# Output stage of an attention and MXFP4 linear layer: VectorE's order and one maximum moved to GpSimd

## What is computed

```python
x = _layernorm(x + _L0_attn_ref(x, ...), axis=-1)          # 32 heads of 16, causal, RoPE, bias, softmax offset
x = _layernorm(x + _L0_ffn_ref(x, ffn_weight, ffn_bias), axis=-1)

def _quant_dequant_mxfp4(x):                               # on blocks of 32 along the last axis
    amax = jnp.max(jnp.abs(xb), axis=-1, keepdims=True)
    exp = jnp.floor(jnp.log2(jnp.maximum(amax, tiny))) - 2.0
    scale = jnp.where(amax > 0, jnp.exp2(exp), 1.0)
    q = jnp.clip(xb / scale, -6.0, 6.0)
    aq = jnp.abs(q)
    lsb = jnp.where(aq < 2.0, 0.5, jnp.where(aq < 4.0, 1.0, 2.0))
    return jnp.round(q / lsb) * lsb * scale

def _L0_ffn_ref(input, weight, bias):
    return quant_dequant(input) @ quant_dequant(weight).T + bias
```

## Time and profile before

| | us |
|---|---|
| median of 3 runs | 1631.46 |
| lowest and highest of them | 1629.03, 1632.43 |
| the profiled execution, its own time | 1629.73 |
| its span, first to last instruction | 1627.9 |

### The profile page before, as it was taken

The page is one execution under the profiler, slowest core; times in us unless marked ns, Lnnn a source line. Parts: engine busy times, 40 slices in busy tenths (PEclk is TensorE's granted clock), DMA queues, the critical chain, the costliest instruction groups (busy, mean ns, idle before and its releaser), DMA issues.

```text
span 1627.9 us, 28334 instructions
## 1 busy us (share of the span) xinstructions
PE 1539.4 (95%) x9552; PEld 813.7 (50%) x9552; DVE 1286.0 (79%) x3828; ACT 1097.2 (67%) x1396; POOL 259.1 (16%) x160
## 2 busy tenths in 40 slices
PE   8999999899999999999999999999999998899984
PEld 6877677444444444444444444444444444444431
DVE  5668988787888887888888888788888776289995
ACT  5544444577777778877778787777777888434542
POOL 6545454300000000000000000000000000033432
PEclk9999999999999999999999999999999999999985
DMA  5695757363335334345423543433453202013221
GB/s 200 196 248 183 196 176 202 115 108 57 48 60 110 57 48 86 51 70 84 69 48 48 106 72 48 81 53 60 70 97 47 47 16 79 26 56 100 78 78 52
DMA packets 129254, 147.57 MB, mean 91 GB/s; under 512 B 48595, under 2 KB 81427, under 8 KB 129110
## 3 DMA queue, kind: packets, MB, share of 16 engines
q1 hardware_dynamic: 129110, 145.76, 40.6%
HBM read 102.32 MB, written 42.60 MB: 89 GB/s over the span
## 4 chain that ended last, share of the span: by engine, by line
PE 71%; DVE 15%; issue 6%; POOL 3%; ACT 2%; DMA 1%; SPq 1%; POOLq 0%; DVEq 0%; ACTq 0%
PE ps L777 17%; PE ps L734 15%; PE ps L754 13%; PE ps L828 11%; PE ps L759 9%; DVE junk L1341 4%; PE ps L947 3%; DVE mx L1334 2%; POOL probs L1287 1%; PE ps L787 1%; DVE stats L1621 1%; DVE probs L1649 1%; DVE work L1519 1%; ACT probs L1070 1%; DVE bias_s L1494 1%
## 5 line engine op out<-in xcount | busy, mean ns | idle before, releaser
L1070 ACT ACTIVATE probs<-ps 128x1024 f32<-128x1024 f32 (+1 forms) x640 | 587.9, 938 | 194.7 <-PE ps L759 98.1
L1341 DVE CUSTOM_DVE_ANT_0 junk<-ps,bias_q 128x384 bf16<-128x384 f32 (+2 forms) x1024 | 502.9, 502 | 108.2 <-PE ps L734 100.4
L734 PE MATMUL ps<-k_stack,q_stack 96*128 96x384 bf16 (+3 forms) x1536 | 440.7, 334 | 24.6 <-DVE mx L1341 11.5
L754 PE MATMUL ps<-q_stack,k_stack 99*128 99x512 bf16 (+3 forms) x1536 | 450.1, 329 | 7.6 <-ACT ps L1085 5.3
L1334 DVE TENSOR_REDUCE mx<-ps 128x1 f32<-128x128 f32 (+3 forms) x768 | 371.2, 487 | 77.4 <-PE ps L734 76.2
L759 PE MATMUL ps<-bias_r,ident_r 128*128 128x384 f32 (+2 forms) x1280 | 337.7, 363 | 0.0
L777 PE MATMUL ps<-probs,v_sb 128*17 128x512 f32 (+3 forms) x3072 | 309.7, 490 | 0.0
L734 PEld LDWEIGHTS ps<-k_stack,q_stack 96*128 96x128 bf16 x1536 | 127.5, 97 | 331.7 <-DVE mx L1341 157.7
L828 PE MATMUL ps<-split 128*128 128x512 f32 x1152 | 284.1, 404 | 9.2 <-POOL split L1223 7.0
L1085 ACT ACTIVATE ps<-bias_s 128x1024 f32<-128x1024 f32 (+2 forms) x320 | 234.5, 746 | 26.3 <-ACT probs L1070 0.8
L828 PEld LDWEIGHTS ps<-split 128*128 128x128 f32 x1152 | 216.0, 190 | 51.3 <-POOL split L1223 7.7
(11 more groups left out here) (125 smaller groups left out, 1086.6 us busy)
## 6 DMA issues: line engine op xcount, KB each, us to landing
q_stack<-q_parts SPq DMA_DIRECT2D x192, 128.0 KB, 4.2
k_stack<-k_parts SPq DMA_DIRECT2D x32, 384.0 KB, 7.4
q_parts<-q_stack SPq DMA_DIRECT2D x84, 128.0 KB, 2.2
k_parts<-k_stack SPq DMA_DIRECT2D x84, 128.0 KB, 2.0
v_dram<-v_sb SPq DMA_DIRECT2D x32, 272.0 KB, 2.6
v_sb<-v_dram SPq DMA_DIRECT2D x32, 272.0 KB, 9.0
k_stack<-k_parts SPq DMA_DIRECT2D x32, 256.0 KB, 8.1
q_stack<-h SPq DMA_DIRECT2D x16, 512.0 KB, 4.2
```

Source lines behind the costliest of these rows:

```text
L734: pe.matmul(ps_ring[:, use.bank, 0:c1 - c0], q_stack[0:STACK, b, hl, I * P:(I + 1) * P], k_stack[0:STACK, b, hl, c0:c1], start=True, stop= ...
L754: mm = pe.matmul(ps_s[:, u % 2, hh, at:at + w], k_stack[0:ROWS, b, hl, J * P:(J + 1) * P], q_stack[0:ROWS, b, hl, i0:i0 + w], start=not in ...
L1070: act.activation(probs[:, (n * NT + u // 2) % 3, 2 * pr:2 * pr + 2, 0:w], ps_s[:, pr, :, 0:w], ACT.Exp).then_inc(exp_done, 1)
L1341: ins = dve.tensor_tensor_reduce(out=junk[:, use.bank, 0:c1 - lo], in0=ps_ring[:, use.bank, lo - c0:c1 - c0], in1=bias_q[:, hl, BAND - t0 ...
```

## The change

Three things, all in the output stage:

- GpSimd gets a new instruction, `at_least_1` (maximum of `mant` with 1, 128x1024 float32, in place), at the head of its iteration, ahead of `unscale_q`. It waits for VectorE's mask; VectorE waits for it (`mant_ready`) ahead of the first of its two remaining rounding sums. VectorE's own maximum (L1517) goes, and `round_steps` counts 3 a step. The preparation of the weight keeps the old `round_step`.
- VectorE's mask comes ahead of the first statistics, right behind `residual1`; nothing stands any more between these statistics and their `moments`.
- VectorE's five scale steps come in one piece ahead of `residual2`, where before they were laid between `residual2`, its statistics, `moments` and `factors`.

```diff
             def unscale_q(s, par):
-                pool.wait_ge(round_steps, s * 4 + 4)
+                pool.wait_ge(round_steps, s * 3 + 3)
...
+            def at_least_1(s):
+                pool.wait_ge(round_steps, s * 3 + 1)
+                pool.tensor_scalar(mant, mant, 1.0, None, ALU.max).then_inc(mant_ready, 1)
...
                 t = at(1)
                 if t.exists:
+                    at_least_1(t.s)
                     unscale_q(t.s, t.par)
...
                     if rd.exists:
+                        q = qs[rd.par]
                         if i == 0:
                             dve.wait_ge(q_scaled, 2 * (rd.s + 1))
                             dve.wait_ge(a_ready, FIRST + rd.s)
-                        round_step(i, qs[rd.par], round_steps, rd.s * 4)
+                            ins = dve.tensor_scalar(mant.bitcast(I32), q.bitcast(I32), MASK, None,
+                                                    ALU.bitwise_and)
+                        elif i == 1:
+                            dve.wait_ge(mant_ready, rd.s + 1)
+                            ins = dve.scalar_tensor_tensor(total, mant, ROUND, q, ALU.mult, ALU.add)
+                        else:
+                            dve.wait_ge(round_steps, rd.s * 3 + 2)
+                            ins = dve.scalar_tensor_tensor(rounded, mant, -ROUND, total, ALU.mult, ALU.add)
+                        ins.then_inc(round_steps, 1)
```

More of the change, by code:

```diff
@@ L488, in build @@
         a_ready = sem("a_ready")
+        mant_ready = sem("mant_ready")
         a_t = sem("a_t")
@@ L1659, in rounding @@
                             dve.wait_ge(a_ready, FIRST + rd.s)
-                        round_step(i, qs[rd.par], round_steps, rd.s * 4)
+                            ins = dve.tensor_scalar(mant.bitcast(I32), q.bitcast(I32), MASK, None,
[7 more added lines that the diff above has]
+                        ins.then_inc(round_steps, 1)
                 if ln.exists:
                     residual1(ln)
+                rounding(0)
+                if ln.exists:
                     dve.wait_ge(y_read, FIRST + W3 * (ln.s + 1))
                     row_stats(0, yv[ln.par], ln1_steps)
-                rounding(0)
-                if ln.exists:
                     moments(0, ln, ln1_steps)
                 rounding(1)
-                rounding(2)
                 if ln.exists:
                     factors(0, ln, ln1_steps, std1)
-                rounding(3)
+                rounding(2)
                 ln, sc = at(0), at(2)
[L1678 to L1681, removed]
+                if sc.exists:
+                    dve.wait_ge(x2_ready, 2 * (sc.s + 1))
+                    for i in range(5):
                         scale_step(i, x2[sc.s % 4], sc.par, q_steps, sc.s * 5)
@@ L1685, in iteration @@
                     residual2(ln)
-                scaling(0)
-                if ln.exists:
                     dve.wait_ge(z_read, FIRST + ln.s + 1)
                     row_stats(1, zv, ln2_steps)
-                scaling(1)
-                if ln.exists:
                     moments(1, ln, ln2_steps)
-                for i in range(2, 5):
-                    scaling(i)
-                if ln.exists:
                     factors(1, ln, ln2_steps, std2)
```

## The result

The changed kernel takes 1653.42 us (median of 4, 1651.99 to 1654.68), the one before 1630.24 beside it: the ratio is 1.014, with a 95% interval from 1.013 to 1.015. It is slower by 23 us. The forecast was 1633.6, with a range up to 1642: right in direction by its centre, far off in size, and outside the range.

A forecast was written before the change was run, and what follows sets the result against it. VectorE, with TensorE close behind, was taken to bound the output stage. Steady iterations went from 11.83 to 12.37 us; with start and end effects that summed to +2.1 us on the 1631.46 median: 1633.6 us, range 1630 to 1642.

The forecast's parts named there:

- GpSimd's maximum at 1.04 us: Output stage, GpSimd: the new maximum priced like its clip of the same shape, 1.04 us, hidden behind VectorE's work.
- the two bare iterations: Iterations 13 and 14, without `residual1` and statistics to hide GpSimd's maximum: mask to first sum 1.86 us each.
- GpSimd's maximum is slow: Rival, 4%: at 1.92 us the first sum waits 0.54 in 12 iterations, 0.88 in two; 1641.8 us.
- Cover of 2.20 us for it, 0.34 to spare: From mask to first sum VectorE has 2.20 us of work; GpSimd's maximum is there after 1.86 us.
- The slots: Steady iteration: VectorE's parts in the new order, priced from trace rows, sum to 12.37 us against 11.83 before.
- That iteration 1 starts at the same time as before: Iterations -3 to 0 are set by TensorE and ScalarE, so iteration 1 starts at 1448.96 in both kernels.
- The stall of L1503 at 0.87: VectorE's 128x32 maximum (old L1497) waits for GpSimd's `unscale_q` each steady iteration: 0.87 us, of which 0.69 is stall.
- No wait ahead of the mask: VectorE's 0.47 us wait for GpSimd ahead of the mask goes: 5.04 us of other work covers the 3.58 needed.
- The fillers as covers of latency: VectorE: instructions between dependent ones hide waits for results; statistics with `moments` directly behind take 1.43 us, 1.20 without the wait.
- Moments beside the clip: Rival, 9%: second `moments` stall beside GpSimd's clip, 0.6 us in 13 iterations, 8 us; 1641.6 us.
- TensorE kept its clock: Rival, 1%: TensorE, busy 11.05 of 12.37 us (89%), loses its clock; time far above everything else.
- TensorE's floor at 11.70: TensorE's transposes lie 11.70 us apart, so a steady iteration can win at most 0.13 us, however much VectorE is relieved.

The follow-up runs named there:

- the fast pair: Changed kernel with GpSimd's maximum written as minimum with 3e38, then maximum with 1: 1631.47 us beside 1630.96 for the kernel before, ratio 1.0008.
- the neighbours' kernel: Separate kernel without the layer: nine more GpSimd forms alone, then small VectorE instructions beside a GpSimd product; four kinds lasted 1.7 to 1.8 us, the others 0.17 to 0.34.

## Why the prediction was wrong, step by step

- **GpSimd's maximum at 1.04 us: wrong, and this is the step that failed.** It took 2.77. In the sum its wait stood at nothing (there after 1.86 us, needed after 2.20); measured, the first sum waits 1.29 us for it in each full iteration. That, 1.72 more than forecast in each of the two bare iterations, and the 1.2 ahead of iteration 1, are nearly the whole miss. The forecast took the nearest row, the clip of the same shape, and for an upper bound the two-source product at 1.92. Both looked at shape and number of inputs; what counts is the pair of operations, and no row of the trace had a single float operation with a constant on GpSimd. The bound was the worse mistake: it was a row of another kind and bounded nothing, so the rival "GpSimd's maximum is slow" (4%, 1641.8 us) was priced at less than half of its true exposure (1.3 us in each iteration and 1.7 in the two bare ones, against 0.54 and 0.88).
- **Cover of 2.20 us for it, 0.34 to spare: right.** With the fast pair the sum didn't wait, and the cover was 2.18.
- **The slots: right.** 12.37 us forecast, 12.28 measured with the fast pair. Two terms were a little large: from the second residual to its statistics 1.19 and not 1.25 (in the changed kernel 1514.84 to 1516.04 is 1.20), and the first sum's slot by 0.03. Over twelve iterations this is 1.1 us too much, against which the one longer iteration adds 0.4; so with the fast pair the stage grew by 1.2 us (219.6 to 220.8) and not by 2.1. That iteration 1 starts at the same time as before was right too for this kernel: 45.69 us behind the stage's first `residual1`, against 45.70.
- **The stall of L1503 at 0.87: right**, in each iteration, and so is its cause: the neighbours' kernel shows which instructions stall and which do not, and moving them away from GpSimd's product removed it. The Trainium skill, SBUF — State Buffer, section "Who interferes with whom", names the same two kinds, and the runs agree on all eight instructions. That it is a port they wait for is the page's account; the runs show only which kinds wait, and until when.
- **No wait ahead of the mask: right** in iterations 1 to 12. The fillers as covers of latency: right too. In the changed kernel moments directly behind their statistics start 1507.90 - 1506.48 = 1.42 us behind them. In the kernel before, an instruction that doesn't need the statistics (L1497, 1543.03 in rows 3) starts 1.20 behind them:

```profile
1541.83 1.28 DVE L1621 BATCH_NORM_STATS2 stats<-probs 128x6 f32<-128x512 f32 x2
```

  I had weighed a sentence of the Trainium skill against this (VectorE: DVE Perf Modes, section "The DRAIN you can't avoid"). It says that a semaphore between two copies costs nothing extra; that dependence costs nothing was my extension of it, and that did not hold here.
- **Rivals.** Moments beside the clip did not stall: L1633 at 1517.47 ran beside GpSimd's clip (1517.38 to 1518.42) in 0.25 us for two, and a single aggregate took 0.17 us beside a product. TensorE kept its clock through nearly all of the steady iterations, a granted 1.00 in the one shown, at 11.00 us busy of 13.70. From 1472 to 1476 us the granted clock averaged 0.57, after TensorE had idled 2.7 us; VectorE did not wait for it. At the end of the stage, with little work left, the granted clock is 0.50 in both kernels (1600 to 1610 us).
- **TensorE's floor at 11.70: right**, and reached (11.69) by the version with the fast pair and the scale steps moved.
- **Direction.** The sign of the centre was right (slower, by 2.1), but that was luck: the reasons behind it are worth at most a tenth of the loss. Of the 23 us, 22 are the form of one instruction. Taken apart: with the maximum on VectorE the reordering costs 10 us; the maximum alone in the fast form costs 5; together in the fast form they cost next to nothing (0.5 us, with an interval from 0 to 3). By the rows that is since the mask, now ahead of statistics and moments, lets these cover the round trip, and since no wait stands ahead of the mask any more.

## What to carry to other kernels

Before work is moved to GpSimd, measure that very instruction there, with its operations and their order: a row of the same shape is no price for it, and a bound has to come from the same kind of instruction. If a single minimum, maximum, sum or product is needed, try to write it as one of the fast pairs with a harmless constant, and time it. For the maximum these runs show it, with a minimum with 3e38 in front, which is harmless as long as no value is larger; for the others no harmless constant was timed. Where a short VectorE instruction can fall beside a long GpSimd one, look at its kind: those with two SBUF inputs and TENSOR_SCALARs waited until GpSimd was done, so lay reductions, statistics or operations with one input from PSUM there instead (the second residual, L1655, took 1.16 us beside `scale_q`, no longer than in the kernel before, 1.22).

## What the runs showed of the hardware that I had not expected

- On GpSimd a TENSOR_SCALAR over 128x1024 in float32 takes 1.04 us for minimum then maximum, product then sum, sum then product and product then product; 2.77 us for one operation of any kind tried (maximum, minimum, product, sum), 1.49 on 128x512; 3.6 us for maximum twice, maximum then minimum, product then maximum and sum then maximum. A copy takes 1.04. Neither the data nor the place nor neighbours changed this by more than 0.02 us. VectorE takes 0.69 for the four forms that were tried on it. Why some pairs are fast isn't shown by these runs; pairs and constants other than these weren't tried.
- The order of the two operations alone is worth 2.6 us: 1.04 for minimum then maximum, 3.63 for maximum then minimum.
- A 128x32 maximum on VectorE lasts 1.83 us beside a GpSimd product and a 128x32 reciprocal 0.34: the kind decides it, not the size.
